# A four-layer graph network on one core: the adjacency cast by GpSimd-issued DMAs to fp8 and to bf16 rows, and each half-row load used for two heads

## The reference

```python
# layer 0: four heads of 64 features
scores = leaky_relu(el[:, :, None] + er.T[None, :, :], 0.2)
scores = where(adj[:, None, :] == 0, -inf, scores)
out = einsum('nhj,jhf->nhf', softmax(scores), ht)
# layer 1: adjacency without its diagonal, a GRU cell on its product with h, and three heads
edge_output = gru_cell(adj_n @ h, h, edge weights)
def head(W, a):                    # e: one score per column, from h @ W, adj_n and a
    att = where(adj_n > 0, e[None, :], -9e15)
    return (softmax(att, axis=1) * adj_n) @ (h @ W)
node_output = gru_cell((head0 + head1 + head2) / 3, h, node weights)
layer1 = de[:, None] * edge_output + dn[:, None] * node_output
# layer 2: mean over neighbours and a linear map; layer 3: weights from entries between 0 and 1
```

## Time and profile before

| | us |
|---|---|
| median of 3 runs | 1352.21 (1351.94 to 1353.33) |
| the profiled execution, its own time | 1358.34 |
| its span, first to last instruction | 1356.5 |

### The profile page before, as it was taken

How to read it: one execution, slowest core, us unless ns; L and a number is a source line. 1 busy time by engine, 2 the same in 40 slices (tenths; PEclk the granted TensorE clock), 3 DMA queues, 4 the chain that set the end, 5 groups by cost and what they waited for, 6 DMA issues and landing times.

```text
span 1356.5 us, 35957 instructions
## 1 busy us (share of the span) xinstructions
PE 1152.5 (85%) x15055; PEld 944.2 (70%) x15055; DVE 974.1 (72%) x2219; ACT 808.2 (60%) x1232; POOL 322.9 (24%) x383
## 2 busy tenths in 40 slices
PE   4519888999867999899867999999899997778996
PEld 3419888999856776566635888887788654436885
DVE  5599897899983576676776999897995364552541
ACT  3468898999752233322326999897889365653000
POOL 4762323133041032333232111111120142220000
PEclk9859999999875999989987999999899998899998
DMA  9733445111026667677779778677752010020532
GB/s 320 241 135 121 176 131 186 35 35 66 3 71 214 198 222 253 211 246 254 272 257 345 228 273 323 220 249 250 263 191 102 5 32 13 18 92 1 192 108 84
DMA packets 89450, 225.10 MB, mean 166 GB/s; under 512 B 7506, under 2 KB 52674, under 8 KB 89026
## 3 DMA queue, kind: packets, MB, share of 16 engines
q1 hardware_dynamic: 88097, 222.21, 48.5%
q10 hardware_dynamic: 1184, 0.53, 0.1%
HBM read 202.98 MB, written 19.73 MB: 164 GB/s over the span
## 4 chain that ended last, share of the span: by engine, by line
PE 49%; DVE 16%; DMA 15%; issue 6%; ACT 6%; POOL 5%; SPq 1%; DVEq 0%; ACTq 0%; POOLq 0%
PE PS L1676 12%; DMA arena<-in_adj 12%; PE PS L1817 10%; PE PS L1818 10%; PE PS L1871 8%; DVE scratch L1372 3%; PE PS L1767 3%; DVE arena L1214 2%; PE PS L1858 2%; DVE arena L1220 2%; DVE arena L1160 2%; PE PS L1774 1%; PE PS L1711 1%; POOL X L738 1%; ACT arena L823 1%
## 5 line engine op out<-in xcount | busy, mean ns | idle before, releaser
L1817 PE MATMUL PS<-arena 128*128 128x257 f16 x1452 | 331.6, 276 | 21.5 <-ACT arena L968 14.9
L1818 PE MATMUL PS<-arena 128*128 128x257 f16 x1452 | 331.4, 277 | 0.0
L1676 PE MATMUL PS<-arena 128*128 128x65 f16 x7744 | 260.9, 196 | 72.3 <-DVE arena L1220 56.9
L1676 PEld LDWEIGHTS PS<-arena 128*128 128x128 fp8e4 x7744 | 257.3, 99 | 75.8 <-issue 59.9
L1372 DVE CUSTOM_DVE_ANT_0 scratch<-arena 128x1408 bf16<-128x1408 f32 x132 | 216.4, 1639 | 78.7 <-DMA arena<-in_adj 46.1
L865 ACT ACTIVATE arena<-arena 128x1024 fp8e4<-128x1024 f32 (+1 forms) x231 | 227.6, 1079 | 21.1 <-DVE arena L1214 20.7
L968 ACT ACTIVATE arena<-arena 128x896 int16<-128x896 uint8 (+1 forms) x198 | 187.3, 971 | 31.9 <-DVE arena L1425 22.4
L1817 PEld LDWEIGHTS PS<-arena 128*128 128x128 bf16 x1452 | 144.3, 99 | 47.5 <-ACT arena L968 13.2
L1818 PEld LDWEIGHTS PS<-arena 128*128 128x128 bf16 x1452 | 141.6, 97 | 23.1
L959 ACT ACTIVATE arena<-arena,E1B 128x896 uint8<-128x896 f32 (+1 forms) x131 | 139.1, 1062 | 13.1 <-DMA arena<-m_rows 13.1
L1214 DVE TENSOR_TENSOR arena<-arena,AT 128x256 int32<-128x256 int32 (+1 forms) x264 | 115.4, 437 | 26.7 <-ACT arena L865 23.8
(11 more groups left out here) (187 smaller groups left out, 1537.6 us busy)
## 6 DMA issues: line engine op xcount, KB each, us to landing
arena<-in_adj SPq DMA_DIRECT2D x176, 704.0 KB, 5.3
arena<-in_adjT SPq DMA_DIRECT2D x44, 512.0 KB, 7.6
hw_saved<-arena SPq DMA_DIRECT2D x22, 387.0 KB, 7.3
arena<-in_adjT SPq DMA_DIRECT2D x22, 384.0 KB, 5.1
arena<-hw_saved SPq DMA_DIRECT2D x9, 774.0 KB, 7.8
arena<-h_saved SPq DMA_DIRECT2D x44, 128.0 KB, 2.1
arena<-e_rows SPq DMA_DIRECT2D x3, 1408.0 KB, 7.3
arena<-el_rows SPq DMA_DIRECT2D x8, 512.0 KB, 5.4
```

Source lines behind the costliest of these rows:

```text
L1676: ins = pe.matmul(PS[:, k, q * C0:(q + 1) * C0], MASK[:, (m + j) % NMASK, q, k * P:(k + 1) * P], MOV[:, j, 2 * h + q, a, :], start=(j == 0 ...
L1817: pe.matmul(PS[:, k, 0:D + 1], weights, w[:, 0:D + 1], start=(j == 0), stop=False)
L1818: ins = pe.matmul(PS[:, k, 0:D + 1], weights, w[:, D + 2:2 * D + 3], start=False, stop=(j == NT - 1))
```

## The change

- **Casts by DMA.** STG, `load_chunk` and POOL's 66 casts go. POOL issues 22 DMAs that read `adjT` as f32 and write group 0 of AT as fp8, all ahead of the weight pieces, and behind the MOV steps 22 more, of 1 MB read each, for groups 1 and 2 together. DVE's first mask of unit 0 and that of unit 4 wait for all 22 of theirs; before, each step waited for its own chunk.
- **bf16 rows.** POOL then issues 22 DMAs from DRAM to DRAM that write `adj` as bf16 into a new tensor `adj_rows_half` (31.7 MB read, 15.9 MB written). SP loads the 22 diagonal blocks (f32, DBLK), POOL clears their diagonals in one instruction and writes them back over the bf16 rows in 22 DMAs. `clear_diagonal` goes. SP waits for all of it (`rows_h`) ahead of the weights of layer 1.
- **One load for two heads.** EB holds the scores of heads 0 and 1 at once. `row_max(i)` for i below 88 takes the half-row i // 2 and the head i % 2; 44 loads of 352 KB serve both, and 44 more serve head 2: 88 loads instead of 132. AROW has two buffers of bf16.
- **Order.** The 88 paired maxima stand in the GRU steps 0 to 19 (`ROWS_LAST` = 20): 4 or 5 for a step, where 3 or 4 stood. The 44 of head 2 stand at m = 8 to 104, about every 2.25 steps. Heads 0 and 1 are turned together in GRU step 20, head 2 at (5, 0), with its MB loaded behind (5, 3).
- The checks use their own three f32 buffers (CROW, over EB and AROW). POOL's share of the exponents, which `first_of` never chose, is deleted.

```diff
-    ROWS_SPLIT = 13
-    ROWS_EDGE = 73
+    ROWS_LAST = 20
...
-        EB = a1.take(N)
-        AROW = a1.take(3, QUARTER)
+        EB = a1.take(2, N)
+        AROW = a1.take(2, QUARTER, dt=BF16, size=2)
...
         def rows_before(t):
...
+            return min(PAIRED, -(-PAIRED * t // ROWS_LAST))
+        def loads_before(t):
+            return max(2, -(-rows_before(t) // 2))
+        row_at = {8 + 9 * i // 4: 2 * NT + i for i in range(2 * NT)}
...
+            sp.wait_ge(sem("rows_h"), 16 * 2 * NT)
...
             def load_row(L):
-                h, t, c = row_of(L)
-                if L >= 3:
-                    sp.wait_ge(sem("rmax"), L - 2)
+                t, c = half_of(L)
+                if L >= 2:
+                    sp.wait_ge(sem("rmax"), maxima_after(L - 2))
+                sp.dma_start(AROW[:, L % 2, :], AH_D[t, :, c * QUARTER:(c + 1) * QUARTER]
...
-            load_scores(EB, 0)
+            load_scores(EB[:, 0, :], 0)
+            load_scores(EB[:, 1, :], 1)
...
             for t in range(NT):
-                pool.wait_ge(sem(f"stg{t % 4}"), 16 * (t // 4 + 1))
-                pool.tensor_copy(AT[:, t, 0:GA[0][1] * P], STG[:, t % 4, 0:GA[0][1] * P], saturate=False
+                pool.dma_start(AT[:, t, 0:GA[0][1] * P], adjT[t, :, 0:GA[0][1] * P]).then_inc(sem("adj_a"), 16)
...
+            for t in range(NT):
+                pool.dma_start(AT[:, t, GA[0][1] * P:NT * P], adjT[t, :, GA[0][1] * P:NT * P]).then_inc(sem("adj_b"), 16)
+            for t in range(NT):
+                pool.dma_start(AH_D[t], t_in["adj"][t * P:(t + 1) * P, :]).then_inc(sem("rows_h"), 16)
+            pool.wait_ge(sem("dblk"), 16 * NT)
+            link(pool.tensor_tensor(DBLK, DBLK, NOTI[:].unsqueeze(1).to_broadcast([P, NT, P]), ALU.mult))
+            pool.wait_ge(sem("rows_h"), 16 * NT)
+            for t in range(NT):
+                pool.dma_start(AH_D[t, :, t * P:(t + 1) * P], DBLK[:, t, :]).then_inc(sem("rows_h"), 16)
...
-                if h == 0:
-                    dve.wait_ge(sem("stg_cast" if g == 0 else "stg_used"), j + 1 + (g - 1) * NT if g else j + 1)
+                if h == 0 and j == 0:
+                    dve.wait_ge(sem("adj_a" if g == 0 else "adj_b"), 16 * NT)
...
-                if n == 5 and j == 15:
-                    save_maxima(2)
+                if n == 5 and j == 2:
+                    save_maxima(2, 1)
```

More of the change, by code:

```diff
@@ L163, in gnn_stack_kernel @@
         HTF = AT[:, :, htf_at:htf_at + 4 * H0 * C0].bitcast(F32)
+        ar = Arena()
+        ar.at = stg_at
+        DBLK = ar.take(NT, P)
+        assert ar.at <= stg_end
         THRi = THR.bitcast(mybir.dt.int32)
@@ L295, in gnn_stack_kernel @@
         banks_before.append(cnt)
-        stg_before = [16 * len(range(q, len(chunk0), 4)) for q in range(4)]
+        stg_before = [0] * 4
         def threshold_on_act(n, j):
@@ L386, in first_of @@
             return 1 if m % 3 == 2 else 0
-        first_count = [[0], [0], [0]]
+        first_count = [[0], [0]]
         for m in range(3 * 3 * NT):
-            for e in range(3):
+            for e in range(2):
                 first_count[e].append(first_count[e][-1] + (first_of(m) == e))
-        first_sem = ["y_act", "y_dve", "y_pool"]
+        first_sem = ["y_act", "y_dve"]
         units1 = [(h, g) for h in range(H1) for g in range(len(G0))]
@@ L474, in _ @@
             load_el(1)
-            for n in range(NT, NT + 4):
-                load_chunk(n)
+            for t in range(NT):
+                sp.dma_start(DBLK[:, t, :], t_in["adj"][t * P:(t + 1) * P, t * P:(t + 1) * P]).then_inc(sem("dblk"), 16)
             for u in range(len(units0)):
                 for j in range(NT):
-                    if (u, j) in casts_at and casts_at[(u, j)] + 4 < len(chunk0):
-                        load_chunk(casts_at[(u, j)] + 4)
                     if j == 20 and u + 2 < len(units0):
@@ L516, in _ @@
                     load_halves(GWS, 0, "we")
-            for L in range(3):
+            for L in range(2):
                 load_row(L)
@@ L545, in load_maxima @@
                 b0, nb = G0[g]
-                sp.wait_ge(sem("mn"), 16 * (h + 1))
+                sp.wait_ge(sem("mn"), 16 if h < 2 else 32)
                 if n >= 2:
-                    for e in range(3):
+                    for e in range(2):
                         sp.wait_ge(sem(first_sem[e]), first_count[e][(n - 1) * NT])
@@ L576, in _ @@
                         load_products(0, c)
-            for L in range(ROWS_EDGE, ROWS_EDGE + 3):
+            for L in range(2 * NT, 2 * NT + 2):
                 load_row(L)
@@ L753, in _ @@
                     delta(t, 0, HR, GT)
-                    for L in range(rows_before(t + 1), rows_before(t + 2)):
-                        clear_diagonal(L)
                 if t >= 1:
```

194 lines of the change are left out of this document (71 added, 123 removed).

## The result

The changed kernel takes 1370.5 us (1368.58 to 1371.67, 4 runs) against 1352.1 (1351.28 to 1353.33) of the kernel before in the same comparison: ratio 1.0111, 95% interval 1.0085 to 1.0138. It is 1.1% slower, where the prediction said 1318. The span is 1369.7 us against 1356.5.

A forecast was written before the change was run, and what follows sets the result against it. No one engine was taken to bound the program; stages were priced separately. The sum 2.8 + 2.4 - 2 + 14.0 + 8 + 9 = 34.2 us gave 1318 for the median; own range 1303 to 1332, the whole one up to 1365.

The forecast's parts named there:

- the row copy: Behind the casts in layer 0: 31.7 MB read in 102 us, done at about 265, covered by some 90 us of room.
- units 4 to 7: Layer 0: without POOL's casts beside DVE these units take 24.1 us each instead of 24.7, a gain of 2.4 us.
- the start: Before POOL's MOV steps: 22 casts and their waits go, 22 DMA issues come; POOL ready at 57.45, a gain of 2.8 us.
- the first GRU: Waits for rows go, steps take 11.3 us instead of 12.3: 19.0 us gained, less a start 5.0 late, net 14.0.
- The casts' price: Layer 0: the 23.1 MB of casting loads run at the plain 310 GB/s, done at 162, 11 us ahead of need.
- the cast halves the rate: Rival: casting loads at 155 or 187 GB/s make DVE stand at unit 4; about 1368 us, chance 0.22.
- d: Cost to POOL of one DMA issue at the start: 0.85 us taken, between 0.33 and 1.53.
- The late clearing of AT: Layer 0: POOL clears AT's diagonal later, beside DVE; 2 us charged, between 0 and 6.
- 4.4 maxima: First GRU: DVE's step with 4.4 maxima takes 10.35 us, just under PE's 10.65, before contention.
- The second load of scores: Start of the first GRU: head 1's scores load behind head 0's, so products(1) starts 5.0 us late.
- Into the attention: Between GRU and attention: gap of 6.2 us instead of 8.4, and 6 us less lost behind it; together 8 us.
- Third head: Start of the attention's third head: maxima turned 13 steps earlier, so 9 of the 9.5 us lost there come back.

The follow-up runs named there:

- experiment 7: The changed kernel with one of its 22 row copies, all later half-row loads reading that one row; 1321.6 us, ratio 0.9762.
- experiment 10: The kernel of experiment 8 plus 11 plain f32 copies of adjacency rows, issued by SP beside units 4 to 7; 1336.0 us, ratio 0.9828.
- experiment 2: The changed kernel with its 22 casting row copies issued one for every 6 masks, from unit 2's first mask on; 1353.8 us, ratio 0.9984.
- experiment 8: The changed kernel with 6 row copies behind the first two el_rows broadcasts, 16 in the GRU, adjacency casts paced, small clears; 1319.0 us, ratio 0.9755.

## Why the prediction was wrong

**The failed step.** It is the one on the row copy: "31.7 MB read, 102 us at 310 GB/s, done at about 265 ... so some 90 us of room cover it". I asked who waits for the row copy, and found nobody before 390. I didn't ask who shares the DMA engines with it. Two did: the broadcasts of `el_rows`, one for each unit (one landed 71.6 us after its issue and held unit 4 up for 44.6), and PE's own instructions. The prediction put the cost of the row copies in layer 0 at nothing; experiment 7 measured 47 us. That is most of the error of 52.5. Without the row copies, or with them elsewhere, the kernel takes 1321.6 and 1319.0 us, against 1318 predicted. That these lie so near is in part luck: below, units 4 to 7 and the start gave 7.5 us more than forecast, and the first GRU 3.6 less.

**The casts' price**, the term I held for the doubtful one, was not the trouble. 23.1 MB of f32 landed in 62 us (87.7 to 149.7), 373 GB/s, faster than the 310 I took; the row copies read 31.7 MB in 75.6 us, 419 GB/s. The rival "the cast halves the rate" has its centre at 1368, close to the measured time, and that is chance. It put low GB/s and a stall at unit 4 forward as its signs, and both were there; but the GB/s of the profile count the bytes written, a quarter of those read (its list has 256 KB for each cast of 1 MB, and 117 GB/s between 88 and 150 us), and the stall was not DVE's for the casts. The sign was badly chosen; the landing time would have told the two apart.

**The start**: a gain of 2.8 forecast with d = 0.85; d is 0.54, the coefficients bound, and 4.9 came. The 3.1 us that the Trainium skill, "SBUF — State Buffer", section "A bandwidth-pool intuition that's wrong (but worth ruling out)", has for a GpSimd DMA that overlaps a DVE copy did not show: the four stretches with 22 issues took 0.50 to 0.56 us for each. But the gain was lost in unit 0. DVE's threshold took 8.55 us instead of 0.61 beside POOL's long clear:

```profile
108.24 8.55 DVE L1142 TENSOR_SCALAR arena<-arena 128x768 fp8e4<-128x768 f32 x1
```

I had named that clear ("one clearing of DBLK") without asking who stands beside it.

**Units 4 to 7**: 2.4 us forecast, 7.8 measured. I laid the difference on POOL's casts. PE's waits point elsewhere: between 181 and 280 us of the kernel before, 9.8 us of "issue"; in units 5 to 7 of after, with little traffic, 0.3. The 9.5 us between them cover the whole gain: the f32 chunk loads had been delaying PE's packets all along. Casts and loads went with the same change, so no run parts the two; but experiment 10 brought back transfers alone, and the stops came back. **The late clearing of AT**: 2 us charged, 0.3 measured.

**First GRU**: net 14.0 forecast, 10.4 measured. In the prediction's own way a step took (743.31 - 510.37 - 11.7) / 19 = 11.6 us, not 11.3. `delta` at 1.53 us, 0.61 of wait behind it (11.0 / 18) and no wait for rows all came as forecast. The mis-sized term is the average: I set 4.4 maxima a step against PE. But a step has 4 or 5. Those with 4 took 10.9 us, near PE's 10.65; those with 5 took 12.7, bound by DVE. I compared the engines' averages; but each step takes the time of the slower engine in that step, and the average of those times is larger. The second load of scores put `products(1)` 2.1 us later, not 5.0 (75.6 us behind the bias load against 73.5), though DVE stood 11.0 us for scores instead of 6.3.

**Into the attention**: 8 forecast, 10.6 measured: 4.0 in the gap (6.2 forecast, 4.4 measured), and in the first 27 us 215 matmuls instead of 155, 60 / 9.1 = 6.6 us (6 forecast). **Third head**: 9 forecast; the attention's 15.9 less 6.6 leave 9.3.

The chance of slower was 0.21, and the upper end of the range, 1365, lay 5.5 us too low.

## What to carry to other kernels

A transfer that nobody waits for still has neighbours: before placing a large one, list every small transfer and every stretch of short matmuls that runs beside it, and price them by the length of its packets. Put bulk copies where TensorE issues few, long matmuls or stands, and let them start behind the small loads that are due. Where the work of a step comes in whole pieces, sum the larger of the two engines for each kind of step, not the averages.

## What the hardware showed

- Large transfers slow TensorE without touching its data. In the changed kernel it stood 1.1 to 2.7 us after nearly every 128 matmuls of 65 columns; in experiment 10 after some multiples of 128, up to 5.2 us. This came with casting and with plain copies, from SP's and from POOL's queue. Each of these stops in the changed kernel (14) and in that of experiment 2 (nine) ended 1.2 to 1.6 us behind the landing of a 16 KB instruction packet.
- Two queues with work moved the same number of packets, 838 each in 60 us, though one moved 15 KB with each and the other 0.5 KB. A broadcast of 64 small packets for each DMA engine took 71.6 us beside large packets of 1.16 us each, 92.1 beside packets of 1.51, and 4.9 to 5.5 us in the kernel of experiment 8 (units 4 to 7).
- A casting DMA issued by GpSimd took 0.50 to 0.56 us of GpSimd, and f32 was read at 373 GB/s to fp8 and 419 GB/s to bf16.
- GpSimd's `tensor_tensor` over 2816 columns shuts out VectorE for all its length (6.14 beside 6.54 us). The Trainium skill, "SBUF — State Buffer", section "Who interferes with whom", says so of VectorE instructions with two inputs in SBUF, as the mask is; the trace agrees.
